# A scan of 512 stages with a mixture of experts beside it: clip first, the FFN's last parts moved into the next block, router steps moved behind `force`

## The reference

```python
def _derivative(q, p, drive, coupling, bias):
    i_couple = jnp.tanh(q) @ coupling.T
    dq = q - q ** 3 / 3.0 - p + drive + i_couple + bias
    dp = EPSILON * (q + ALPHA - BETA * p)
    return (dq, dp)
...
    q_next = q + DT / 6.0 * (dq1 + 2 * dq2 + 2 * dq3 + dq4)
    p_next = p + DT / 6.0 * (dp1 + 2 * dp2 + 2 * dp3 + dp4)
    q_next = jnp.clip(q_next, -CLAMP, CLAMP)
    p_next = jnp.clip(p_next, -CLAMP, CLAMP)
...
    probs = jax.nn.softmax(logits.astype(jnp.float32), axis=-1)
    rw, sel = jax.lax.top_k(probs, TOP_K)
    combine = jnp.zeros((T, E), x.dtype).at[jnp.arange(T)[:, None], sel].add(rw)
    sh = _silu_and_mul(x @ Ws_gate_up, I_SH) @ Ws_down
    shared_out = sh * jax.nn.sigmoid(x @ W_sgate.T)
    gu = jnp.einsum('th,ehi->eti', x, We_gate_up)
    h = _silu_and_mul(gu, I_MOE)
    eo = jnp.einsum('eti,eih->eth', h, We_down)
    sparse_out = jnp.einsum('eth,te->th', eo, combine)
    return (shared_out + sparse_out).reshape(orig_shape)
```

## Time and profile before

| | |
|---|---|
| median of 3 runs | 729.99 us (729.94 to 730.53) |
| the profiled execution: its time, its span | 729.92 us, 728.1 us |
| TensorE matmuls busy | 662.3 us (91%), 12101 instructions |
| VectorE busy | 675.7 us (93%), 4624 instructions |
| ScalarE busy | 431.8 us (59%), 2310 instructions |
| GpSimd busy | 175.2 us (24%), 372 instructions |
| warm matmuls (L536) | 1245 |
| granted TensorE clock | 1.0 over the whole span |
| chain that ended last | PE 44%, DVE 43%, ACT 5%, issue 4% |

### The profile page before, as it was taken

The page is one execution under the profiler, slowest core; times in us unless marked ns, Lnnn a source line. Parts: engine busy times, 40 slices in busy tenths (PEclk is TensorE's granted clock), DMA queues, the critical chain, the costliest instruction groups (busy, mean ns, idle before and its releaser), DMA issues.

```text
span 728.1 us, 32965 instructions
## 1 busy us (share of the span) xinstructions
PE 662.3 (91%) x12101; PEld 598.1 (82%) x12101; DVE 675.7 (93%) x4624; ACT 431.8 (59%) x2310; POOL 175.2 (24%) x372
## 2 busy tenths in 40 slices
PE   2537999999999999999999999999999999999998
PEld 1326888988889898888888888898888888888888
DVE  5899999999999999999999999999999999999972
ACT  3866656566564655656565665656656565655643
POOL 0001231313222131322223222221322222132234
PEclk9999999999999999999999999999999999999999
DMA  8600000000000000000000000000000000000000
GB/s 313 205 2 2 3 3 11 4 9 4 10 3 3 10 3 10 4 10 4 3 11 3 10 3 11 2 4 10 3 10 4 11 3 3 10 4 10 4 9 9
DMA packets 8626, 13.60 MB, mean 19 GB/s; under 512 B 1520, under 2 KB 7984, under 8 KB 8208
## 3 DMA queue, kind: packets, MB, share of 16 engines
q1 hardware_dynamic: 8464, 11.50, 4.6%
HBM read 9.40 MB, written 2.10 MB: 16 GB/s over the span
## 4 chain that ended last, share of the span: by engine, by line
PE 44%; DVE 43%; ACT 5%; issue 4%; DMA 2%; SPq 0%; POOL 0%; DVEq 0%; POOLq 0%
PE down_ps L520 17%; PE up_ps L506 8%; PE coup_ps L455 7%; PE coup_ps L448 7%; DVE hidden L776 6%; DVE th_lo L684 4%; DVE force L706 4%; DVE p_part L622 4%; DVE cubic L687 3%; DVE p_sum L642 3%; DVE q_raw L718 3%; PE warm_ps L536 2%; DMA wf<-in_w_up 2%; DVE base L663 2%; DVE w L617 2%
## 5 line engine op out<-in xcount | busy, mean ns | idle before, releaser
L506 PE MATMUL up_ps<-q_hi,w 128*128 128x128 f16 x2176 | 224.7, 219 | 0.6 <-POOL q_lo L807 0.6
L448 PE MATMUL coup_ps<-th_hi,c 128*128 128x16 f16 x4096 | 182.3, 171 | 26.7 <-ACT th_hi L347 23.3
L506 PE MATMUL up_ps<-q_lo,w 128*128 128x128 f16 x1088 | 195.5, 219 | 0.0
L448 PEld LDWEIGHTS coup_ps<-th_hi,c 128*128 128x128 f16 x4096 | 148.7, 97 | 55.8 <-ACT th_hi L347 44.6
L837 POOL TENSOR_TENSOR hidden<-hidden,comb_s 128x128 f32<-128x128 f32 x272 | 123.8, 457 | 290.9 <-DVE force L706 243.8
L347 ACT ACTIVATE th_hi<-q 128x32 f16<-128x32 f32 x384 | 88.0, 229 | 174.7 <-DVE q L718 172.9
L506 PEld LDWEIGHTS up_ps<-q_hi,w 128*128 128x128 f16 x2176 | 173.8, 97 | 0.8 <-POOL q_lo L807 0.7
L455 PE MATMUL coup_ps<-th_lo,c 128*128 128x16 f16 x2048 | 131.8, 173 | 29.6 <-DVE th_lo L684 24.4
L520 PE MATMUL down_ps<-hidden,wd 128*128 128x128 f32 x1088 | 157.8, 285 | 0.0
L455 PEld LDWEIGHTS coup_ps<-th_lo,c 128*128 128x128 f16 x2048 | 85.9, 97 | 62.6 <-DVE th_lo L684 42.0
L520 PEld LDWEIGHTS down_ps<-hidden,wd 128*128 128x128 f32 x1088 | 133.3, 191 | 0.0
(11 more groups left out here) (87 smaller groups left out, 919.5 us busy)
## 6 DMA issues: line engine op xcount, KB each, us to landing
wf<-in_w_up SPq DMA_DIRECT2D x1, 4224.0 KB, 13.3
wd<-in_w_down SPq DMA_DIRECT2D x1, 2048.0 KB, 22.4
out<-out_s SPq DMA_DIRECT2D x16, 128.0 KB, 2.1
xs<-in_x SPq DMA_DIRECT2D x1, 1920.0 KB, 18.4
sel<-in_spread SPq DMA_DIRECT2D x1, 408.0 KB, 18.1
...
```

Of the source, the lines that this page charges most:

```text
L448: nc.tensor.matmul(coup_ps[:, m * B:(m + 1) * B], c16[:, part, k, m * P:(m + 1) * P], th_hi[:, k, :], start=part == m == k == 0, stop=Fals ...
L506: last = nc.tensor.matmul(up_ps[j % 4][:, h * TOK:(h + 1) * TOK], w16[:, part, k, h, j * P:(j + 1) * P], q[:, k, :], start=n == 0, stop=n ...
```

## The change

Six things change.

- In a stage with k = 0 the clip is VectorE's first instruction (behind `p_part`), ahead of `rest1`. `rest2` moves from the end of k = 0 into k = 1, ahead of `p_sum`; `base3` moves from ahead of `th_lo` to behind `cubic`, and `base4` from there to behind `force`.
- The FFN's tables are new. Its pieces now run from stage 0 to stage 45, so that FFN f = b - 2 (at st + 32) and FFN f = b - 1 (at st) share the stages of block b. In stages 0 to 13 of a block the last eight down products and five weighs of the older FFN, its last copy and its `out_s` stand beside the start of the younger one. After block 15 the tail holds what is left of FFN 14 and all of FFN 15.
- Router steps 3, 5 and 6 stand behind `force`, in stages 6, 8 and 10 (`ROUTE_LATE`, called by `late()`), and `top`, `shifted` and step 4 in stages 2, 3 and 7.
- `q_lo` is made in two halves, in stages 0 and 1.
- GpSimd waits for `summands` only in stages where it has a piece (`POOL_AT`).
- `WARM` subtracts what the older FFN fills, the router's product counted as a down product, and is issued from block 1 on as before.

```diff
-UP_AT = [st for st in range(3, 25) if st % 4 != 2]
-SILU_AT = [s + 1 for s in UP_AT]
-HIDE_AT = [s + 2 for s in UP_AT]
-SPREAD_AT = [12, 15, 18, 22, 26]
+HIDE_AT = [5, 6, 10, 14, 15, 17, 18, 19, 21, 22, 23, 25, 26, 27, 29, 30, 31]
+SILU_AT = [s - 1 for s in HIDE_AT]
+UP_AT = [s - 2 for s in HIDE_AT]
+TURN_AT = 13
+SPREAD_AT = [15, 19, 23, 27, 31]
...
-WEIGH_AT = list(range(13, 30))
-DOWN_AT = [14, 18, 18, 22, 22, 25, 26, 26, 27, 27, 28, 28, 29, 29, 30, 30, 31]
+WEIGH_AT = [16, 17, 18, 20, 21, 22, 24, 25, 26, 28, 29, 30, 34, 37, 38, 40, 41]
+POOL_AT = {0, 1, 3, 10, 11, 12, *WEIGH_AT}
+DOWN_AT = [18, 18, 22, 22, 26, 26, 30, 30, 31, 33, 33, 34, 37, 39, 39, 41, 42]
+FINISH_AT = [STAGES + 11, STAGES + 13]
...
-WARM = [6, 10, 11] + [max(0, 13 - 12 * UP_AT.count(st) - 8 * DOWN_AT.count(st) - 4 * SPREAD_AT.count(st))
-                      for st in range(3, STAGES)]
+WARM = [max(0, 13 - 12 * UP_AT.count(st) - 8 * (DOWN_AT + [0]).count(st) - 8 * DOWN_AT.count(st + STAGES)
+            - 4 * SPREAD_AT.count(st)) for st in range(STAGES)]
...
-ROUTE_AT = {1: (0, 1), 2: (2,), 4: (3,), 5: (4,), 6: (5,), 7: (6,)}
-FINISH_AT = [2, 3]
+ROUTE_AT = {1: (0,), 2: (1,), 3: (2,), 7: (4,)}
+ROUTE_LATE = {6: (3,), 8: (5,), 10: (6,)}
...
+        def ffn_stages(b, st):
+
+            return [(f, at) for f, at in ((b - 2, st + STAGES), (b - 1, st)) if 0 <= f < BLOCKS]
+
+        def tail_stages():
+
+            return [x for st in range(FINISH_AT[-1] + 1) for x in ffn_stages(BLOCKS, st)]
...
                 if k == 0:
 
                     if t:
-                        dve.wait_ge(p_clipped, t)
+                        dve.wait_ge(q_ready, n)
+                        if i == 1 and b:
+                            dve.wait_ge(q_split, (KC + 1) * b)
+                        nc.vector.tensor_scalar(q, q_raw[:], CLAMP, -CLAMP, ALU.min, ALU.max).then_inc(q_clipped, 1)
                     nc.vector.tensor_tensor(rest[0][:], drive[:, t, 0], p_now[:], ALU.subtract
                                             ).then_inc(rest1_ready, 1)
-                    if t:
-                        dve.wait_ge(q_ready, n)
-                        if i == 1 and b:
-                            dve.wait_ge(q_split, 2 * b)
-                        nc.vector.tensor_scalar(q, q_raw[:], CLAMP, -CLAMP, ALU.min, ALU.max).then_inc(q_clipped, 1)
...
                 nc.vector.tensor_tensor(force[:], rest[k][:], cubic[:], ALU.subtract).then_inc(summands, 1)
-                if k == 0:
-
-                    dve.wait_ge(based, t + 1)
-                    nc.vector.scalar_tensor_tensor(rest[1][:], q, R2_Q1, base[:, 0, :].rearrange(
-                        "p (m b) -> p m b", m=KC), ALU.mult, ALU.add).then_inc(rested, 1)
+                late()
+                if k == 1:
+
+                    nc.vector.scalar_tensor_tensor(base4[:], q0_of(i), R4_Q1, base[:, 2, :].rearrange(
+                        "p (m b) -> p m b", m=KC), ALU.mult, ALU.add).then_inc(based_q, 1)
...
-                if st == 0:
-
-                    pool.wait_ge(q_split, 2 * f + 1)
-                    nc.gpsimd.tensor_tensor(q_lo[:], q_trace[:].rearrange("p m t b -> p m (t b)"), q_hi[:],
+                if st < KC:
+
+                    pool.wait_ge(q_split, (KC + 1) * f + 1)
+                    nc.gpsimd.tensor_tensor(q_lo[:, st], q_trace[:, st].rearrange("p t b -> p (t b)"), q_hi[:, st],
                                             ALU.subtract).then_inc(q_split, 1)
```

102 lines of the change are left out of this document (55 added, 47 removed).

## The result

The changed kernel takes 698.09 us (median of 4 runs, 697.48 to 698.65); the kernel before, in the same series, 730.18 (4 runs, 729.94 to 730.53). The ratio is 0.956, with a 95% interval of 0.9543 to 0.9577. The profiled execution took 698.65 us, with a span of 696.8.

What follows compares the result with a forecast made beforehand. It saw a chain of 512 stages, 82% in steady blocks. Saving 2.32 a block gave 32.5 over fourteen, plus 2.0 (block 1) and 0.5 (block 0), less 3.2 (tail): 31.8 off 729.99, so 698.1; 8 in 10 for 694.5 to 704.

Steps and rivals of the forecast that it cites:

- Clip first: k = 0 stages: an earlier clip frees ScalarE's square, stages become 1.24; 0.08 each in stages 0, 8, 12, 0.24 a block.
- Weighs off k = 3: Stages 16, 20, 24, 28: no weigh starts in them, so they become 1.24; 1.12 a block, 0.20 each from p_part.
- Down products: Pairs in stages 18, 22, 26, 30 without spread or up tile: stages 19 and 23 gain 0.32 together.
- Router: Router steps moved: stages 4 and 5 gain 0.33, stage 7 0.33, stage 1 0.18; stage 10 costs 0.26, stage 6 0.03.
- Tail: After the last stage: eight more down products, the turn at 9.0; the tail grows by 3.2 to 29.6.
- The rule weighed against the trace: GpSimd's expo beside stages 4 and 5: the skill's port lock would make stage 4 near 2.4, but the trace disagrees.
- Rival 2: expo or a half of q_lo blocks VectorE in its new stage: 715 us; chance 0.03.
- GpSimd's dropped waits cost nothing either way, since it idles there.: GpSimd's waits in stages without a piece: dropping them was valued at nothing.
- rest2 leaves the end of the k = 0 stage: rest2 moves to the front of k = 1, off the path; with clip first, 0.5 gain in block 0.
- Rival 1: Work behind force delays q: base4 by 0.11 in every k = 1 stage, 13 us, 711; chance 0.10, with partial cases.
- Block 1: Block 1 gains 2.0, between 0.5 and 2.8; some up tiles may stay slow as the new table issues fewer warm matmuls.
- I take 1.28: Stages behind down pairs: coupling at +0.76 or +0.79, stage 1.25 to 1.28; 1.28 taken, 27 and 31 staying.

Runs made afterwards that it cites:

- experiment 1: Changed kernel with the clip back behind rest1, nothing else undone: 706.76 us.
- experiment 3: Changed kernel with three weighs one stage earlier (19, 23, 27), so that they run beside p_part in stages 20, 24, 28: 706.11 us.
- experiment 4: Changed kernel with the spreads of groups 1 to 4 one stage earlier, ahead of the down pairs in stages 18, 22, 26, 30: 705.93 us.
- experiment 8: Changed kernel with GpSimd waiting for the summands in every stage again, with a piece or without: 707.1 us.
- experiment 12: Kernel before, with GpSimd waiting for the summands only in stages with a piece: 727.48 us, against 729.9 for the kernel before.
- Experiment 2: Changed kernel with rest2, base3 and base4 back in their old places, the clip staying first: 698.02 us.
- experiment 5: Changed kernel with block 1's warm matmuls counted without the older FFN's down products, which block 1 doesn't have: 696.71 us.
- experiment 9: Changed kernel with block 1's fuller warm matmuls, first and second earlier in the tail, and stage 0's wait for driven moved behind force of stage 31: 695.01 us.
- experiment 6: Changed kernel with first and second ahead of hidden tile 2 in the tail: 696.29 us.
- experiment 7: Changed kernel with router steps 3, 5 and 6 in VectorE's slot of stages 6, 8 and 10 instead of behind force: 704.27 us.
- experiment 11: Changed kernel with a never-blocking wait, on a semaphore reached at set-up, in each of GpSimd's stages without a piece: 705.7 us.
- experiment 10: Kernel of experiment 9 without its tail edit, with first and second in the slot of stage 9: 696.4 us.

## Why the prediction was right, and where it wasn't

698.1 was forecast and 698.09 measured. The model held: a stage is as long as the later of th_lo's path, the square's path and TensorE's filling makes it. But some steps failed, and their misses nearly cancel.

Right, and shown:
- *Clip first*: 0.08 or 0.09 for each stage whose square it frees, 0.03 in stage 0 (experiment 1).
- *Weighs off k = 3*: 0.18 a stage for the weigh beside p_part, 0.20 forecast (experiment 3). Stages 16, 20, 24, 28 are 1.23 or 1.24.
- *Down products*: 1.44 with the spread, 1.25 without (experiment 4).
- *Router*: stages 4 and 5 at 2.47 (2.48 forecast), stage 7 at 1.24 (1.25), stage 1 at 1.26 (1.30), first and second 0.27 behind force (0.26). Stage 6 at 1.27 holds total and best for 0.03, as forecast.
- *Tail*: +3.01 against +3.2, the turn at 8.8 against 9.0.
- *The rule weighed against the trace*: expo locked nothing out. It lasts 1.64 us in stage 4, and base, which reads two SBUF operands, takes 0.26 under it; a lock until expo's end would have held base until +1.67. The Trainium skill (SBUF — State Buffer, "Who interferes with whom") has a VectorE instruction with two SBUF inputs contend with any GpSimd instruction that reads SBUF. The weigh behaves so here (p_part 0.41 instead of 0.22 in experiment 3), expo doesn't. Rival 2 fell with that row, and with stages 1 and 2, which hold the halves of q_lo, at 1.26 and 1.27.

Wrong:
- *"GpSimd's dropped waits cost nothing either way, since it idles there."* This is the step that failed. Put back as experiment 8 has them, two a stage, they cost 9.0 us, over a quarter of the gain; one a stage would cost 1.6 by the estimate there. The sum still came out because it took +0.04 for every weigh as given, from the earlier trace rows, a weigh that follows weighs. In the kernel as written that was true only thanks to the part that it valued at nothing. Stage 14's 0.11, booked under "the weigh that stood beside its rest3", was the same cost: experiment 12 removes it by the waits alone, and the weigh stays in that stage.
- *"rest2 leaves the end of the k = 0 stage", and with it 0.5 in block 0.* Block 0 is as long as before: its stages 4 and 16 fell from 1.32 to 1.23 and 1.27, the other k = 0 stages stayed, and the first q came 0.18 later. Experiment 2, with rest2 back, has the same two stages at 1.23 and 1.27, and shows that the move gains nothing in the steady blocks either. What freed the square in the k = 0 stages is the clip's place alone. Rival 1, the price of base4 behind force, is refuted by the k = 1 stages: q follows force by 0.23 in stage 5 of block 7, with base4 between.
- *Block 1*: 1.06 instead of 2.0. WARM there subtracts down products that don't exist. The forecast saw it and took too little for it; 0.65 comes back in experiment 5, and 1.06 + 0.65 = 1.71.
- *"I take 1.28" behind pairs*: 1.25 or 1.26. The next coupling product starts at +0.75, just under the lower of the two values that the forecast named. In the four stages for which it took 1.28 (19, 23, 27 and 31) that is 0.10 a block to the good. Against it stage 0 is 1.29, not 1.24: its clip comes at +0.36, behind the wait for `driven`. That the wait is the cause rests on experiment 9, which moved both.
- *The steady block*: 10 of the 14 are 40.12 to 40.14, 0.17 under the forecast's 40.3, which would be 2.4 us in 14 blocks. The mean is 40.30 all the same, because single blocks are longer: block 4 by 1.7, block 2 by 0.3, block 5 by 0.2, block 10 by 0.1. And the sum was made from block 7 of before (42.60), while the mean of the 14 was 42.68: 0.8 more gain than the forecast's 32.5.

Block 4 has a cause of its own, in windows over its stage 0 and its stages 2 and 3 (q alone; the fourth number is the granted clock):

```profile
183.53:185.17 1.64, 0.25 (x1) 1.00 0.00 0
186.44:190.33 3.89, 0.50 (x3) 0.56 0.00 0
```

and VectorE's timeline in that stage 0:

```profile
184.24 0.18 DVE L666 TENSOR_SCALAR q_trace<-q_raw 128x32 f32<-128x32 f32 x1 [0.33 <-issue]
```

The clip comes 0.71 behind q_raw, with an idle time that no semaphore ends. Stage 0 takes 1.64; TensorE idles 0.39 in it ahead of the low coupling product, and one stage later the granted clock falls to a mean of 0.56, close to its lower level of 1.2 GHz. A pair of down products takes 1.90 there instead of 1.14, and stages 2 and 3 take 2.05 and 1.84. The late clip is in the same place in the profiles of experiments 2 to 8 and 11 (stage 0 of 1.63 or 1.64), but the fall of the clock only in that of experiment 7. So the late clip doesn't suffice for it. In the other kernels the clip of this one stage is late too, but by less: +0.53 or +0.54 where +0.40 is usual in the kernel before and in experiments 1 and 12, with rest1 between the wait for `driven` and the clip, and +0.43 where +0.30 is usual in experiments 9 and 10, with the wait gone from stage 0. So 0.13 to 0.15 comes whatever the kernel, and 0.35 where the wait stands right ahead of the clip. What sets it, and whether the unprofiled runs fall too, stays open.

So the match to 0.01 us is luck in its last digits. By spans, 31.3 came where 31.8 was forecast: 0.5 short in block 0, 0.9 short in block 1, 0.8 over in the 14 blocks, 0.2 better in the tail (the parts are rounded); and the median lies 0.56 under the profiled execution. The four runs lie in two pairs, at 697.48 and 697.62 and at 698.56 and 698.65, and the median falls between them, where no run lies. The gain was in the stages where it was expected.

**Left open.** What a met wait costs GpSimd goes with its place behind the wait that is met last, in nearly all weighs of five kernels (experiment 11), but that was read from them afterwards, and the order of the waits was not varied by itself. One wait a stage in the changed kernel was not run either.
